# Turning a token block with 32x32 transposes on VectorE and a trip through DRAM, with VectorE scaling it

## What is computed

```python
proj = einsum('bsd,ed->bse', x, in_proj_w)          # gate, hBC, dt
hBC  = silu(conv(hBC))                              # 4 taps along the tokens
hs   = hBC[..., :INTER].reshape(b, s, H, P)
xch  = (hs * dt[..., None]).reshape(b, nc, CHUNK, H, P)
Y_diag = einsum('bzlhn,bzshn,bhzls,bzshp->bzlhp', Cc, Bc, L, xch)
states = einsum('bzlhn,bhzl,bzlhp->bzhpn', Bc, decay_states, xch)
Y_off  = einsum('bzlhn,bzhpn,bhzl->bzlhp', Cc, prev, exp(A_cum))
Y = Y_diag + Y_off + hs * D
out = rmsnorm_by_group(Y * silu(gate)) * norm_w @ out_proj_w.T
```

## Time and profile before

| | |
|---|---|
| time, median of 3 runs | 1598.37 us (1598.18 to 1598.73) |
| span of the profiled execution | 1596.2 us |
| busy share of the span | PE 99%, PEld 81%, DVE 84%, ACT 77%, POOL 77% |
| granted TensorE clock | at its upper level in all 40 slices |
| DMA, share of 16 engines | 34.2% on SyncE's queue, 178.69 MB in all |

### The profile page before, as it was taken

How to read it: one execution, slowest core, us unless ns; L and a number is a source line. 1 busy time by engine, 2 the same in 40 slices (tenths; PEclk the granted TensorE clock), 3 DMA queues, 4 the chain that set the end, 5 groups by cost and what they waited for, 6 DMA issues and landing times.

```text
span 1596.2 us, 27397 instructions
## 1 busy us (share of the span) xinstructions
PE 1577.7 (99%) x9112; PEld 1299.6 (81%) x9112; DVE 1347.6 (84%) x1878; ACT 1230.8 (77%) x2391; POOL 1224.1 (77%) x1013
## 2 busy tenths in 40 slices
PE   8999999999999999999999999999999999999998
PEld 6878888888888888888888888888888888888865
DVE  6787898879979799787988889887998879978797
ACT  5888778886778877787877877878777886878864
POOL 4578788787797868878687787878688786787864
PEclk9999999999999999999999999999999999999999
DMA  3643424233242322333234332433334333342411
GB/s 116 200 157 108 130 83 153 87 115 108 87 145 96 123 100 100 129 100 109 87 115 140 99 123 74 131 118 92 116 101 136 102 102 106 100 149 77 142 60 60
DMA packets 88156, 178.69 MB, mean 112 GB/s; under 512 B 16592, under 2 KB 20688, under 8 KB 87760
## 3 DMA queue, kind: packets, MB, share of 16 engines
q1 hardware_dynamic: 87008, 176.77, 34.2%
q10 hardware_dynamic: 1008, 0.17, 0.1%
HBM read 172.17 MB, written 4.72 MB: 111 GB/s over the span
## 4 chain that ended last, share of the span: by engine, by line
PE 94%; DVE 1%; POOL 1%; ACT 1%; issue 1%; DMA 0%; SPq 0%; POOLq 0%; DVEq 0%; ACTq 0%
PE proj L514 16%; PE proj L516 16%; PE proj L515 16%; PE p_yd L690 8%; PE p_out L562 7%; PE p_out L564 7%; PE p_out L563 7%; PE p_st L571 5%; PE p_hid L526 4%; PE proj L626 2%; PE p_st L702 1%; PE p_st L700 1%; PE p_st L701 1%; PE p_misc L537 1%; PE p_misc L583 0%
## 5 line engine op out<-in xcount | busy, mean ns | idle before, releaser
L514 PE MATMUL proj<-x_hi,w_hi 128*128 128x512 f32 x1160 | 462.0, 398 | 7.6 <-DVE x_lo L1323 7.0
L515 PE MATMUL proj<-x_lo,w_hi 128*128 128x512 f32 x1160 | 452.9, 390 | 0.0
L516 PE MATMUL proj<-x_hi,w_lo 128*128 128x512 f32 x1160 | 452.9, 390 | 0.0
L1034 POOL TENSOR_TENSOR w_lo<-raw,w_hi 128x512 fp32r<-128x512 f32 x209 | 284.2, 1364 | 101.8 <-ACT w_hi L754 99.3
L1198 DVE SCALAR_TENSOR_TENSOR hs<-proj,uch,hs 128x511 f32<-128x511 f32 (+2 forms) x384 | 285.4, 743 | 42.4 <-ACT hs L781 37.5
L842 ACT ACTIVATE decay<-decay,tok 128x128 f32<-128x128 f32 x1024 | 312.4, 391 | 0.0
L514 PEld LDWEIGHTS proj<-x_hi,w_hi 128*128 128x128 f32 x1160 | 218.8, 189 | 53.2 <-issue 11.2
L516 PEld LDWEIGHTS proj<-x_hi,w_lo 128*128 128x128 f32 x1160 | 218.3, 188 | 46.2
L515 PEld LDWEIGHTS proj<-x_lo,w_hi 128*128 128x128 f32 x1160 | 218.9, 189 | 42.2
L1227 DVE TENSOR_TENSOR decay<-decay,cb 128x1024 f32<-128x1024 f32 x128 | 199.0, 1555 | 56.0 <-ACT decay L860 54.3
L1092 POOL TENSOR_TENSOR dh<-dh,eac 128x512 f32<-128x512 f32 x96 | 127.2, 1325 | 144.0 <-DVE eac L1258 140.3
(11 more groups left out here) (139 smaller groups left out, 3037.6 us busy)
## 6 DMA issues: line engine op xcount, KB each, us to landing
decay<-acum_d SPq DMA_DIRECT2D x128, 512.0 KB, 4.4
raw<-w_t SPq DMA_DIRECT2D x209, 256.0 KB, 2.9
eac<-eacum_d SPq DMA_DIRECT2D x192, 128.0 KB, 3.0
wo_raw<-wo_t SPq DMA_DIRECT2D x32, 256.0 KB, 4.0
c_new<-wo_t SPq DMA_DIRECT2D x32, 256.0 KB, 4.2
hs<-x_t SPq DMA_DIRECT2D x8, 256.0 KB, 5.7
acc<-x_tok SPq DMA_DIRECT2D x8, 256.0 KB, 3.1
out<-acc SPq DMA_DIRECT2D x8, 256.0 KB, 2.0
```

Source lines behind the costliest of these rows:

```text
L514: nc.tensor.matmul(dst[:], w_hi[:, ws, k, :], x_hi[:, k, cols], start=(k == 0), stop=False)
L515: nc.tensor.matmul(dst[:], w_hi[:, ws, k, :], x_lo[:, k, cols], start=False, stop=False)
L516: mm = nc.tensor.matmul(dst[:], w_lo[:, ws, k, :], x_hi[:, k, cols], start=False, stop=(k == KC - 1))
L1034: nc.gpsimd.tensor_tensor(w_lo[:, s].rearrange("p a b -> p (a b)"), raw[:, s, :], w_hi[:, s].rearrange("p a b -> p (a b)").bitcast(F32), A ...
```

## The change

For c = 1 to 7 of each unit (112 of 128 steps) TensorE no longer turns the block. For c = 0 all stays as it was. Instead:

- VectorE, `turn_blocks`, two steps ahead: one transpose instruction over the 128 x 512 block turns each 32 x 32 piece in place, into `x_blk`. The pieces then still have to change places between partitions.
- SyncE, `store_blocks`: one DMA of 256 KB from `x_blk` to the DRAM buffer `turned_d`. `load_blocks`: four DMAs of 64 KB, each to 32 partitions of `x_tok_sb`, in runs of 512 bytes.
- VectorE, `scale_tokens`, one step ahead: `xdt` is `x_tok_sb` times `dt_blk`, with both inputs in SBUF.
- GpSimd, `lay_dt`, once a unit: two copies that lay out the time steps as `dt_blk`.
- The scratch space of GpSimd's DMAs is cut to 1024 bytes, which makes room for the new tiles.

The core of the diff:

```diff
@@ sync @@
+            def store_blocks(g, e, c):
+
+                n = turn_n(g, e, c)
+                sp.wait_ge(blocks_turned, n)
+                wait(sp, x_here, 64 * (n - 2))
+                sp.dma_start(turned_d[n % 2].rearrange("i a n -> (i a) n"),
+                             x_blk[:].rearrange("p q j b -> p (q j b)")).then_inc(blocks_stored, 16)
+
+            def load_blocks(g, e, c):
+
+                n = turn_n(g, e, c)
+                sp.wait_ge(blocks_stored, 16 * n)
+                wait(sp, x_here, 64 * (n - 1))
+                wait(sp, xdt_ready, step(g, e, c) - 1)
+                for q in range(UT):
+                    sp.dma_start(x_tok_sb[q * BLK:(q + 1) * BLK, n % 2].rearrange("a i j b -> a i (j b)"),
+                                 turned_d[n % 2, :, :, q * P:(q + 1) * P].rearrange("i a n -> a i n")).then_inc(x_here, 16)
...
                         if not (last and od):
                             load_decay(sp, g + od, ed, cd)
+                        o2, e2, c2 = ahead(e, c, 2)
+                        if c2 and not (last and o2):
+                            store_blocks(g + o2, e2, c2)
                         for t in tiles_of(e, c, last):
                             off, n = divmod(t.n + 4, GRP_TILES)
                             if not (last and off):
                                 load_tile(g + off, LOOP_TILES[n], last)
+                        if c2 and not (last and o2):
+                            load_blocks(g + o2, e2, c2)
@@ tensor, front @@
-                wait(pe, xdt_ready, step(g, e, c))
-                if c == 0 or c == CPB:
-                    pe.wait_ge(hs_ready, 8 * u + (8 if c else 7 if u else 4))
-                for j in range(UT):
-                    mm = nc.tensor.transpose(p_hid[:, 2 * j:2 * j + 2, :].rearrange("p a b -> p (a b)"),
-                                             hs[:, e, j, c * P:(c + 1) * P], ident[:])
-                mm.then_inc(hid_ready, 1)
+                if c == 0:
+                    wait(pe, xdt_ready, step(g, e, c))
+                    pe.wait_ge(hs_ready, 8 * u + (7 if u else 4))
+                    for j in range(UT):
+                        mm = nc.tensor.transpose(p_hid[:, 2 * j:2 * j + 2, :].rearrange("p a b -> p (a b)"),
+                                                 hs[:, e, j, c * P:(c + 1) * P], ident[:])
+                    mm.then_inc(hid_ready, 1)
@@ gpsimd @@
+            def lay_dt(u):
+
+                g, e = u // 2, u % 2
+                if g:
+                    pool.wait_ge(unit_loaded[e], 48 * g + 32)
+                wait(pool, xdt_ready, 8 * u)
+                for r in range(2):
+                    nc.gpsimd.tensor_copy(dt_blk[:, :, r::2, :], tok[:, e, 1].rearrange("p c (j q) -> p c q j", j=UT)).then_inc(dt_blk_ready, 1)
...
+                        if c == 7 and not (last and off):
+                            lay_dt(2 * g + e + 1)
@@ vector @@
             def front(g, e, c):
 
-                dve.wait_ge(hid_ready, step(g, e, c) + 1)
-                wait(dve, xd_scaled, carried(g, e, c))
-                nc.vector.tensor_tensor(xdt[:], p_hid[:], bcast(tok[:, e, 1, c, :], 2, HD), ALU.mult).then_inc(xdt_ready, 1)
+                if c == 0:
+                    dve.wait_ge(hid_ready, 2 * g + e + 1)
+                    wait(dve, xd_scaled, carried(g, e, c))
+                    nc.vector.tensor_tensor(xdt[:], p_hid[:], bcast(tok[:, e, 1, c, :], 2, HD), ALU.mult).then_inc(xdt_ready, 1)
...
+            def scale_tokens(g, e, c):
+
+                dve.wait_ge(x_here, 64 * turn_n(g, e, c))
+                dve.wait_ge(yd_ready, step(g, e, c))
+                wait(dve, xd_scaled, carried(g, e, c))
+                if c == 1:
+                    dve.wait_ge(dt_blk_ready, 2 * (2 * g + e + 1))
+                nc.vector.tensor_tensor(xdt[:].rearrange("p h d -> p (h d)").rearrange("p (j i b) -> p i j b", j=UT, i=UT),
+                                        x_tok_sb[:, turn_n(g, e, c) % 2], bcast(dt_blk[:, c], 3, BLK), ALU.mult).then_inc(xdt_ready, 1)
+
+            def turn_blocks(g, e, c):
+
+                u = 2 * g + e
+                wait(dve, blocks_stored, 16 * (turn_n(g, e, c) - 1))
+                dve.wait_ge(hs_ready, 8 * u + (8 if c >= CPB else 7 if u else 4))
+                nc.vector.transpose(x_blk[:], hs[:, e, :, c * P:(c + 1) * P].rearrange("p j (q a) -> p q j a", q=UT)
+                                    ).then_inc(blocks_turned, 1)
...
                         if more:
                             front(g + off, ne, ncn)
+                        if c < 7:
+                            scale_tokens(g, e, c + 1)
+                        o2, e2, c2 = ahead(e, c, 2)
+                        if c2 and not (last and o2):
+                            turn_blocks(g + o2, e2, c2)
                         if tiles:
                             tap(g, tiles[0], 1, 2)
```

14 lines of the change are left out of this document (13 added, 1 removed).

## The result

The changed kernel takes 1642.57 us, the median of four runs (1641.28 to 1648.02), beside 1598.46 us for the kernel before (four runs, 1598.18 to 1598.73). The ratio is 1.028, with a 95% interval of 1.027 to 1.030. The prediction had 1620 us, range 1588 to 1650: the sign was right, but the loss of 44.1 us is about twice the 21.6 us forecast.

The account below looks back on a forecast made before the run. TensorE was taken as the bound, jointly with VectorE at three places a group. Stretches summed to +2.5 us a group, 17.5 in seven, with the last group 21 us: span 1617.5, forecast 1620 us, range 1588 to 1650.

Parts of the forecast that it names:

- stretch B: 796.2 to 868.8 us, (1,5) to (0,3): TensorE saves four turns, -2.4 us, late blocks add 1.3, together -1.1 us a group.
- the pairs: VectorE's added transpose and dearer product in each turned step: 0.62 + 0.16 = 0.78 us more on its queue.
- A: 754.0 to 796.2 us, (1,1) to (1,5): three pairs, 2.34 us, less idle time and margin, +0.9 us a group.
- C: 868.8 to 901.2 us, (0,3) to (0,6): three pairs, 2.34 us, less 0.2 and 0.25 us, +1.9 us a group.
- late blocks: Loads for c = 1 wait behind the second weight tile on SyncE's queue: 1.3 us late in (0,1), 1.5 in (1,1).
- D: 901.2 us to the next 754.0: late blocks and pair of (1,1), 2.3 us, less 1.49 us idle, +0.8 us.
- three tight places: carried_out of (1,4), p_st of (1,5) and (0,6): VectorE just in time, margins 0.06, 0.39, 0.25 us; both engines bound.
- a collision each time: Each product waits out half of a GpSimd split: 0.6 us more instead of 0.16, the sum some 22 us higher.
- The third: Rival: VectorE's pair dearer, by a 1.02 us transpose or colliding product, 1642 us either way, both 1664 us; chance 0.18.
- The first: Rival: TensorE stays the bound everywhere, 1598 - 66 = 1532 us; chance 0.04.
- second: Rival: VectorE's idle time moves and hides the costs, -1.4 us a group, 1588 us; chance 0.18 for faster.
- The fourth: Rival: the store ahead of weight tiles on SyncE's queue delays them, 40 us more, 1660 us; chance 0.03.

## Why the prediction was right in sign and half in size

**By terms.** In the forecast's sum of 21.3 us stand -19 us for the turns (stretch B, 2.4 us, eight times), +24.5 us for the pairs (A 0.9 us seven times, C 1.9 us eight times, 3 us in the last unit) and +16 us for late blocks (B 1.3 us eight times, D 0.8 us seven times, which holds the pair of (1,1) less idle time too). The table above has -10.1, +36.5 and +12.6 us in their places, and +5.2 us for which the sum had nothing. So the loss was missed by 9 us in the turns, 12 us in the pairs and 5 us in the first unit, and overstated by 3 us in the late blocks.

**What bounds.** Right, and not carried far enough. The margins of 0.06, 0.39 and 0.25 us in the earlier trace rows were read as three tight places with free stretches between them. The windows of the earlier trace rows, VectorE 60.38 of 72.60 us, made stretch B look free. A busy share says nothing on where the idle pieces lie: in the kernel without turns A, B, C and D shrink by 0.3, 0.1, 0.9 and 0.1 us. B, where I had counted 2.4 us of gain, gives the least, and C, which I had called tight, the most. This is the first step that failed: 19 us of TensorE's savings were counted, 10.2 us came, and beside the costs 4.3 us.

**The turn.** 0.59 us a step was 0.41 us; the issue gap stays with the next instruction. 66 us in all were 46 us, 8.3 us a group 5.7 us.

**The transpose.** 0.68 us forecast, 0.70 us measured; within the bounds. Added alone it lengthens A by 1.2 us, where three of 0.70 us less the 1.42 us that I had as hidden give 0.7 us.

**The product.** 0.16 us more forecast, 0.26 us measured in the changed kernel and 0.48 us alone. The second step that failed, and a choice that I made openly: the mean of L1251 against a collision each time. L1251 stands where GpSimd is often idle, and 43 of its 128 splits lie beside it for nine tenths of their time or more; those took 1.08 us on average in the trace of before. The product stands in front of GpSimd's `xd`, where 84 of 112 lie so. The row's mean was the mean of another place. The Trainium skill ("SBUF — State Buffer", "Who interferes with whom") says that a VectorE instruction with two SBUF inputs contends with GpSimd's reads, and one with at most one does not. The traces agree on both, 0.68 to 1.74 us against 0.68 to 0.69 us. The prediction took from it an alternative of 22 us; the swap of the source measured 10 to 16 us.

**GpSimd.** Missed. The product from SBUF slows GpSimd too, by 43 us of busy time in the changed kernel, and TensorE waits for it directly in (1,1) and (1,4); the prediction costed one side of it.

**The late block.** The mechanism was right, to the queue and the tile behind which it stands. Forecast 1.3 and 1.5 us of lateness, measured 1.6 to 2.7 and 2.4 to 4.9 us; worth 10.0 us in all, where the forecast's terms for it come to 16. The remark that it would come in no other steps was nearly right: short waits of 0.2 to 1.3 us stand in (0,2) and (1,6) of some groups.

**The first unit.** Missed: 4.5 of the 5.2 us of its row in the table. The first block's store stands behind a weight tile that waits for GpSimd, which is the mechanism of the late blocks once more, at the one place where the prediction did not look for it.

**By stretches**, as forecast and as measured: A +0.9 and 0.0, B -1.1 and +1.6, C +1.9 and +0.6, D +0.8 and +2.5 us. The group was to grow by 2.5 us and grew by 4.7 us, and A and C cost less than forecast. The excess is in B and D, the two in which blocks come late. With the loads earlier B is 0.9 us shorter and D only 0.3 us, so the late block is not the whole of it. A part of it is only the border between D and A, VectorE's first B tap, which itself moves when VectorE is late.

**The rivals.** The third, a dearer pair at 1642 us, had the right mechanism in one of its two forms, the collision, but that it names the measured number is luck: it adds 22 us for the collision alone, where the whole pair was 12 us dearer than forecast, and the rest came from gain that never arrived and from the first unit. The first and second fall with the kernel without turns: even with all costs gone the time is 1588 us. The fourth falls in its size: TensorE does wait for a weight tile, 1.6 to 1.7 us in (1,1) of each group, but behind GpSimd's split and not behind the store, as up to 1.6 us are left with the trip gone.

**What would show it.** TensorE busy 95%, VectorE 88% against "near 90%", waits before carried_out and p_st of (1,5) and p_st of (0,6) for VectorE, the wait for blocks once a unit: all there. But the longest waits for blocks were 4.9 us and not 2, the product row read 0.94 us and not 0.84, and groups of 193 us were 195.4 us.

## What to carry to other kernels

When an engine at 99% is never seen to wait, that doesn't mean that its work can be taken away at a gain: take the work away in one run before anything is built to replace it, as the bound of the gain was 10 us here and what was built in its place cost 54 us. Price an operation by rows at the same place beside the same neighbours, not by a mean over the span; for a VectorE operation, see what GpSimd does at that time, and count GpSimd's loss too. And a load that was added behind waits on a shared queue belongs ahead of them if its reader is nearer than theirs; so, by the trace of the first unit, does its store.

## What the runs showed of the hardware

- A transpose of 128x512 fp32 in 32 x 32 pieces on VectorE took 697 to 707 ns, about as long as a product of that shape from PSUM (681 ns), and didn't slow beside GpSimd.
- A product with both inputs in SBUF took 676 to 1743 ns beside GpSimd and 0.69 us where GpSimd was idle. GpSimd was busy 43 us longer for 112 of them, and even GpSimd's operation on one column a partition (`rs`) went from 632 ns in the kernel before to 1037 ns on average in the one with the product from SBUF alone.
- The issue gap of 0.17 us behind p_yd does not belong to the turn; with the turn gone it stands before the next weight load.
- TensorE's clock fell to half for 3.4 us (once for 6.8 us) at waits of 1.5 to 3.4 us, in some groups and not in others with the same wait: behind the 1.5 us before p_st of (0,6) in two groups of eight. A drop of 3.4 us cost 1.6 us beside the wait.
